# First router's stage: experts' second weights loaded in sixteen pieces instead of four, and nine edge-row buffers instead of five

## What is computed

```
shared = gelu(x @ W1s + b1s) @ W2s + b2s
rw = softmax(x @ Wr);  topw, topi = top_k(rw, 2);  topw = topw / sum(topw)
h = gelu(einsum('bsd,edf->bsef', x, W1p) + b1p)          # 8 experts, 256 -> 1024
priv = einsum('bsef,efd->bsed', h, W2p) + b2p            # 1024 -> 256
out = shared + einsum('bsed,bse->bsd', priv, mask(topw, topi))
...
msg = relu(x[src] + edge_attr)                           # next layer
agg = zeros_like(x).at[dst].add(msg)
```

## Time and profile before

| | us |
|---|---|
| median of 3 runs | 5833.78 |
| lowest and highest | 5833.64, 5835.69 |
| span of the profiled execution (its own time, first to last instruction) | 5848.9 |
| fused stage in it | about 944 to 1203 |
| expert stage in it | about 1203 to 1678 |

### The profile page before, as it was taken

One profiled execution on the slowest core, in us unless ns is written; L12 is line 12 of the kernel. 1 busy time (PEld: TensorE's weight loads), 2 busy tenths in 40 slices (PEclk: granted clock), 3 DMA queues, 4 the chain that ended last, 5 costly groups with the idle time before them and its releaser, 6 DMA issues. The chain is left out here.

```text
span 5848.9 us, 84745 instructions
## 1 busy us (share of the span) xinstructions
PE 4430.2 (76%) x19486; PEld 2881.7 (49%) x19486; DVE 3572.8 (61%) x12025; ACT 1825.6 (31%) x6462; POOL 3575.6 (61%) x3819
## 2 busy tenths in 40 slices
PE   4668786868977777659589966888597588877768
PEld 3333335768853334434355534666496333345536
DVE  9987654411036775543466667888524688867775
ACT  0000002223323333212423335555143355544421
POOL 3767775676657775565577755776123477756620
PEclk9986667989976666755899988999698799999978
DMA  1053336688746775023254447888275388876500
GB/s 54 25 165 102 104 105 166 216 261 253 242 151 203 207 206 141 17 77 103 67 133 127 127 91 230 278 284 260 104 214 147 114 230 231 230 192 189 169 18 23
DMA packets 534429, 914.71 MB, mean 156 GB/s; under 512 B 101969, under 2 KB 384544, under 8 KB 525504
## 3 DMA queue, kind: packets, MB, share of 16 engines
q0 software_dynamic: 164160, 449.94, 28.0%
q1 hardware_dynamic: 309354, 330.73, 18.3%
q10 hardware_dynamic: 60438, 128.64, 7.2%
HBM read 739.18 MB, written 169.76 MB: 155 GB/s over the span
## 5 line engine op out<-in xcount | busy, mean ns | idle before, releaser
L1021 PE MATMUL bank<-small 128*125 128x256 f32 x1660 | 820.2, 616 | 276.4 <-DVE small L988 168.3
L969 POOL DMA_INDIRECT small<-tabA,idxD x830 | 803.1, 968 | 276.2 <-issue 187.1
L1021 PEld LDWEIGHTS bank<-small 128*125 128x125 f32 x1660 | 373.5, 278 | 722.1 <-issue 415.6
L2907 POOL DMA_INDIRECT small<-tabC,idxD x415 | 410.4, 989 | 190.7 <-SPq L202 64.5
L1554 DVE COPY small<-bank 128x256 f32<-128x256 f32 x176 | 74.8, 425 | 736.4 <-PE bank L1609 736.4
L803 POOL DMA_INDIRECT recs<-pkS,rowS x391 | 384.8, 984 | 227.4 <-issue 98.5
L2645 POOL DMA_INDIRECT big<-tabB,idxD x415 | 395.5, 953 | 198.0 <-issue 88.9
L2432 POOL DMA_INDIRECT big<-tabT,idxS x415 | 413.5, 996 | 139.6 <-issue 107.2
L1000 DVE TENSOR_TENSOR big<-big,bank 125x256 f32 x830 | 347.4, 419 | 230.0 <-PE bank L1021 213.8
L2985 PE MATMUL bank<-big,cst 128*125 128x512 f32 x830 | 425.5, 594 | 0.5 <-ACT big L2972 0.5
L1598 PE MATMUL bank<-small,big 128*128 128x128 f32 (+1 forms) x3040 | 414.5, 296 | 0.0
(11 more groups left out here) (484 smaller groups left out, 10191.3 us busy)
## 6 DMA issues: line engine op xcount, KB each, us to landing
big<-in_L_w ACTq DMA_DIRECT2D x56, 1024.0 KB
small<-eaS SPq DMA_DIRECT2D x415, 128.0 KB
eaS<-small SPq DMA_DIRECT2D x415, 128.0 KB, 3.0
big<-eaS SPq DMA_DIRECT2D x415, 128.0 KB, 3.0
big<-in_L2f_w ACTq DMA_DIRECT2D x64, 512.0 KB
big<-rowsD SPq DMA_DIRECT2D x104, 256.0 KB, 4.0
ytab<-small ACTq DMA_DIRECT2D x176, 128.0 KB
big<-rowsS SPq DMA_DIRECT2D x52, 256.0 KB
```

The costliest lines, as they stand in the source:

```text
L969: g.indirect_dma_start(out=self.gb[k % self.RG], out_offset=None, in_=K.tabA, in_offset=row_index(K.idxD, k)).then_inc(*self.got.up(k))
L1021: p.matmul(self.K.bank[k % 4][0:PT, 0:D], self.oh[k % self.RO][:, 0:PT], self.gb[k % self.RG], start=True, stop=True).then_inc(*self.summe ...
L2907: g.indirect_dma_start(out=self.gb[k % self.RG], out_offset=None, in_=K.tabC, in_offset=row_index(K.idxD, k)).then_inc(*self.got.up(k))
```

## The change

`EdgeRows.NB` goes from 5 to 9, with four new buffers of their own, named `edge`. With that, step c loads into buffer c mod 9 and waits for the scatter of step c - 9; the calls that ask for steps are as they were. In the fused stage the experts' second weights, 8 MB in all, are loaded in 16 pieces of 512 KB (1024 columns, half an expert), one at the head of each of the tiles 1 to 16, where there were four loads of 2 MB at the heads of the tiles 1, 7, 13 and 19. The other routers keep their loads.

```diff
-    NB = 5
+    NB = 9
...
         self.buf = [K.idxS[:, 0:D].bitcast(F32), K.locS[:, 0:D], K.wiS[:, 0:D].bitcast(F32), K.eaB[:, :], K.eidD[:, 0:D].bitcast(F32)]
+        self.buf += [K.sb(f"edge{i}", [128, D])[:, :] for i in range(self.NB - 5)]
...
         self.every = max(1, (T - 1) // self.n_w)
+        if shared:
+            self.n_w = E * self.w2 // 1024
...
             s.wait_ge(*self.hid[0].n(t + 1))
-            i = t // self.every
-            if t % self.every == 1 and i < self.n_w:
-                lo, hi = i * self.step, min((i + 1) * self.step, E)
-                s.dma_start(self.w2s[:, lo * self.w2:hi * self.w2].rearrange("p (e c) -> p e c", c=self.w2),
-                            a[self.key + "w"].rearrange("p (e c) -> p e c", c=self.ecols)[:, lo:hi, self.w2off:]).then_inc(*self.weights.up)
+            if 1 <= t <= self.n_w:
+                at = (t - 1) // 2 * self.ecols + self.w2off + (t - 1) % 2 * 1024
+                s.dma_start(self.w2s[:, (t - 1) * 1024:t * 1024], a[self.key + "w"][:, at:at + 1024]).then_inc(*self.weights.up)
             self.side.edges.sync(s, 7 if t % 2 else 6)
```

## The result

The changed kernel takes 5764.26 us (median of four runs, 5762.32 to 5771.2); the kernel before took 5834.73 (median of the three runs above and one more). The ratio is 0.9878, with a 95% interval from 0.9865 to 0.9891: 70 us less by the medians and 71 by the ratio, against a forecast of 75. A ratio here is estimated from all runs and is not exactly the quotient of the medians.

What follows compares the result with a forecast made beforehand. POOL, waiting for edge rows not yet loaded, was taken to end the fused stage and pace the expert stage. Terms -37 and -38 make -75 us, from the median 5833.8 to 5759 us; range 5740 to 5804.

Steps and rivals of the forecast that it cites:

- The bound: Fused and expert stages: POOL ends the first and paces the second, with 44.1 and 43.6 us of waits for loads.
- The expert term: Expert stage: nine buffers outlast the 14.45 us turn, so nearly all of POOL's 43.6 us of waits go; -38 us.
- two close engines: Expert stage: PE at 7.25 us a tile and POOL at 7.61 still trip over each other; 5.6 us kept for it.
- The fused term: Fused stage: with sixteen pieces and nine buffers POOL no longer waits behind second-weight loads; -37 us, bounds 15 and 44.1.
- PE's gate: Fused stage: SP loads tile 8's edges only after PE's first hidden half, so POOL stands there at 1020.5 to 1025.
- the signs: Both stages: among others, no POOL wait over 3 us behind a piece, PE's expert-stage gather stalls under 10 us.
- The rule on small loads: Fused stage: the skill wants 1 MiB per DMA; by its fit sixteen pieces cost 24 us more, sum 51 not 75.
- The terms at nothing: Sorting stage and behind the first layer's gathers: POOL's waits get shorter but POOL is early there, so no gain.
- B: Expert stage: loads are late whenever issued, so extra buffers don't help; only the fused stage gains, 5797 us; chance 0.15.
- C: Fused stage: pieces cost more, turns exceed 11.5 us by 1.4; fused gain 15, sum 53, 5781 us; chance 0.10.
- D: Expert stage: more loads in flight delay gathers, PE stalls more; slower, 5853 us at 20 further stalls; chance 0.05.
- E: SP's loads: held by PE's hidden half, not by buffers; gains under 12 us, 5828 us; chance 0.04.

Runs made afterwards that it cites:

- one-stage runs: Changed kernel, but edge loads wait for the scatter five steps back, in the expert stage only (ratio to the kernel before 0.9935) or the fused stage only (0.9929).
- second profile: The changed kernel, unaltered, run and profiled again in the last session: ratio 0.9867 to the kernel before.
- no piece ahead: Against the changed kernel, all sixteen pieces are issued by SP after its last edge load of the fused stage; ratio 0.9899 to the kernel before.
- balanced version: Against the changed kernel, edge steps and 18 source scatters moved from fused and expert tiles to where POOL is early; 5735.45 us beside 5767.12.

## Why the prediction was right, point by point

**The bound: right.** That POOL's waits for edge rows end the fused stage and pace the expert stage was read from the order of time alone, and each of the one-stage runs gave back the time of that stage, with those waits.

**The expert term, -38: measured -41.6** by the trace of the change, and -38.0 by its second profile. The turn of 14.45 us against what the buffers last was the right sum: five (12.7) wait, six (15.2) wait 8.5 us in the whole stage, nine (22.8) never. The 5.6 us kept back for two close engines were 3.6 too many in the one profile and right in the other. POOL itself lost nothing in either (412.5 us from its first gather to its last DMA in both, 412.1 worked out); in the second profile PE waited 14.1 us within the stage instead of 10.5 and ended later.

**The fused term, -37: measured -38.3, but a part of it was wrong.** The step that failed is the turn of a buffer with a piece in it. It was taken as 8.7 to 11.2 us, that is 6.4 and a piece's 2.35 to 4.85, and so inside the 11.5 us of nine buffers: "I take no wait". In the tiles 4, 5 and 6 such a turn took 12.2, 13.3 and 14.1 us, and POOL's waits were 1.1, 1.4 and 1.9. The one of tile 5, and behind it the same load in the kernel with no piece ahead:

```profile
984.76 0.96 POOL L880 DMA_INDIRECT eaS<-idxS,rowE  x1 [0.30 <-issue]
990.34 0.44 SPq L1360 DMA_DIRECT2D big<-in_L_w  x1
990.82 0.50 SPq L892 DMA_DIRECT2D idxS<-in_ea  x1
998.06 0.96 POOL L880 DMA_INDIRECT eaS<-idxS,rowE  x1 [1.43 <-DMA idxS<-in_ea]
```

```profile
988.70 0.33 SPq L892 DMA_DIRECT2D idxS<-in_ea  x1
993.48 0.96 POOL L880 DMA_INDIRECT eaS<-idxS,rowE  x1 [0.97 <-DMA idxS<-in_ea]
```

Less the usual 0.30, the load was ready 6.9 us after its issue behind a piece, and 4.5 us without. So in this pair the piece cost it some 2.4 us, the low end of what was taken, although a piece itself takes longer to land:

```profile
L1360 SPq DMA_DIRECT2D big<-in_L_w x16: 328/432/1442, 954.3 to 1083.0; - x16
```

```profile
DMA to landing us min/median/max: 3.7/5.8/7.0
```

What was too small is the 6.4: it was read at the end of the stage, where PE had stopped, and here the reload alone left 6.1 us after the scatter. With five buffers, which last 6.4 us, such turns make POOL wait nearly everywhere, which is why pieces alone did nothing. With nine, the pieces cost 4.1 us in the first eight tiles, shown by the run without them, and nothing behind; why the turn fits there is not shown. The prediction laid all that is lost up to tile 8 to PE's gate, for which it had 1020.5 to 1025; without pieces it is 1020.0. That the time at tile 8, 1023.5 forecast and 1025.2 measured, came out near is luck in part; from the first scatter it is 71.0 forecast and 74.2 measured.

The term did not say, either, which edit brings what. The buffers alone bring 27.9 us of it.

Two of the signs that the prediction named were missed by little: a wait of 3.60 us behind a piece (4.58 in the second profile) where none over 3 was to be, and PE's waits within the expert stage, 10.5 and 14.1 us where under 10 were named.

**The rule on small loads.** The Trainium skill (DMA: Bandwidth & Descriptors, "Rules for kernel authors" and "Anatomy of one DMA") speaks for large loads, and by an estimate from its fit sixteen pieces, one after another, are 24 us dearer than four loads. The fit is for software-generated DMAs, and for these loads of SP the measurement decides: 512 KB landed after 5.8 us where it gives 3.2. The fused stage ended 38 us earlier with nine buffers and sixteen pieces than before, and 8 to 10 earlier than with four loads and the same nine buffers. What an estimate of loads one after another leaves out is that nothing here waits for a piece but the loads queued behind it, and behind tile 8 those have buffers' time to spare.

**The terms at nothing: right.** POOL's last scatter of the sorting stage came 7.1 us earlier and the one behind the first layer's gathers 5.1, and the meetings there only 0.4 and 1.1 us: covered, as worked out.

**The rivals.** B fell with the run that has five buffers in the expert stage only; C, since the fused stage gained 38 and not 15; D, since PE's waits for gathered rows fell from 39.4 to 10.5 us (14.1 in the second profile) at 277 GB/s; E, since nine buffers alone gain 61.

**The sum, -75: measured -71** by the ratio, with an interval from 64 to 79, and 5764 us against 5759. By the two profiles it would be 88: about 80 by the end of the expert stage, 8 behind it. The prediction took the difference from the profile of before and the level from its median; the 15 us by which that profile lay above the median were left alone, which was right: single runs of the same kernel lay between 5824 and 5861 in these sessions. Where in that one execution the 15 us stood is not settled, beyond the later stages' few.

## What to carry to other kernels

Where one engine waits for loads that another engine issues, write down one turn of a buffer (use, reload, landing) and how long the buffers last at the consumer's pace; waits vanish nearly at once where the second exceeds the first, and further buffers bring little. Read the turn where the wait is: at the end of the fused stage it was under 6.4 us, in its first tiles over 12 with a piece. Splitting a large transfer ahead of such loads pays only with buffers that bridge each piece. Once the waits are gone, ask who ends the stage now: here it was the same engine, by its work and not its waits, and moving 30 of its DMAs to places where the trace showed it idle brought 32 us more, while moving twelve of them, six to a place behind a wait on the issuing queue, brought none.

## What the runs showed of the hardware

A quarter of the bytes took more than half the time: 512 KB land 5.8 us after their issue, 2 MB 9.4 (10.2 with nine buffers), both among other loads. To a 128 KB load issued right behind it, a 512 KB piece cost some 2.4 us in the one pair above. Sixteen such pieces in one burst took up to 24.5 us each:

```profile
DMA to landing us min/median/max: 4.2/12.8/24.5
```

The granted clock was lower where PE stalled more. Its mean over the expert stage, between the two levels of 2.4 and 1.2 GHz, was 0.94 where PE had stopped for 39 us in sixteen stalls, 0.97 with 10.5 us of them, and 0.98 in the balanced version, where PE waited for no gathered row once it had begun (each window holds some 7 us of idle time ahead of PE's first block):

```profile
1153.00:1562.00 409.00, 401.68 (x2769) 376.52 (x2770) 41.67 (x174) 150.08 (x505) 310.85 (x323) 0.98 0.87 284
```
